# Scores' factor by Ln and Exp instead of Tanh and Square, fewer row copies, and another order of work between attention and experts

## What is computed

```python
qh, kh, vh = proj(q, Wq, bq), proj(k, Wk, bk), proj(v, Wv, bv)
scores = jnp.einsum('bhqd,bhkd->bhqk', qh, kh)
norm_q = jnp.linalg.norm(qh, axis=-1)
norm_k = jnp.linalg.norm(kh, axis=-1)
D_udps = (norm_q[..., :, None] + norm_k[..., None, :]) ** 2
scores = alpha * 4.0 * scores / D_safe          # D_udps, or inf where it is 0
attn = jax.nn.softmax(scores, axis=-1)
...
# experts: the best 2 of 8 for each token, weights by softmax
h = jax.nn.gelu(jnp.einsum('btd,edh->ebth', x, W1) + b1[:, None, None, :], approximate=False)
y = jnp.einsum('ebth,ehd->ebtd', h, W2) + b2[:, None, None, :]
out = jnp.einsum('ebtd,bte->btd', y, dispatch)
x = x + attention(layernorm(x), ctx, ctx); x = x + experts(layernorm(x))
```

## Time and profile before

| | |
|---|---|
| median of 3 runs | 966.4 us (966.29 to 967.87) |
| profiled execution | 970.74 us, of it 968.9 us in the profile's span |
| granted TensorE clock, mean | 0.977 of full |
| TensorE busy | 898.1 us, 93% |
| VectorE, ScalarE, GpSimd busy | 697.2, 634.5, 415.5 us |

### The profile page before, as it was taken

How to read it: one execution, slowest core, us unless ns; L and a number is a source line. 1 busy time by engine, 2 the same in 40 slices (tenths; PEclk the granted TensorE clock), 3 DMA queues, 4 the chain that set the end, 5 groups by cost and what they waited for, 6 DMA issues and landing times.

```text
span 968.9 us, 30634 instructions
## 1 busy us (share of the span) xinstructions
PE 898.1 (93%) x10701; PEld 789.8 (82%) x10701; DVE 697.2 (72%) x1833; ACT 634.5 (65%) x1236; POOL 415.5 (43%) x540
## 2 busy tenths in 40 slices
PE   3999999998999999989899699899999999999994
PEld 2788887787877877878777589799999999999993
DVE  7677888777987887779768577766666666666662
ACT  3688887787877877878857356455555455554551
POOL 6344456538546565385253532623222232222322
PEclk9799999999999999999979799999999999999998
DMA  5222122314132333253044773443333233332222
GB/s 150 70 72 89 41 83 80 112 41 128 57 99 76 126 123 103 92 171 111 20 139 134 275 273 52 85 93 52 51 52 51 47 52 52 52 51 48 46 30 22
DMA packets 61892, 84.82 MB, mean 88 GB/s; under 512 B 9872, under 2 KB 55312, under 8 KB 59568
## 3 DMA queue, kind: packets, MB, share of 16 engines
q1 hardware_dynamic: 47504, 64.26, 21.0%
q0 software_dynamic: 13296, 18.00, 11.1%
q10 hardware_dynamic: 944, 0.60, 0.2%
HBM read 49.86 MB, written 31.92 MB: 84 GB/s over the span
## 4 chain that ended last, share of the span: by engine, by line
PE 74%; issue 7%; DVE 6%; ACT 6%; POOL 3%; another core or an unknown queue 1%; DMA 1%; DVEq 0%; POOLq 0%; ACTq 0%
PE s_ps L711 10%; PE u_ps L711 10%; PE pv_ps L729 9%; PE gen L729 9%; PE gen L502 5%; PE gen L495 5%; PE s_ps L485 5%; PE u_ps L473 3%; PE pv_ps L519 2%; PE gen L544 2%; ACT pt L827 2%; PE gen L415 2%; PE gen L680 2%; PE gen L418 2%; PE gen L422 1%
## 5 line engine op out<-in xcount | busy, mean ns | idle before, releaser
L1567 POOL DMA_INDIRECT out<-yw,rb x71 | 110.3, 1553 | 269.4 <-DVE yw L1392 253.4
L928 ACT ACTIVATE h<-s_ps,b1t,inv 128x128 f32<-128x128 f32 x288 | 107.8, 457 | 89.6 <-PE s_ps L711 79.3
L928 ACT ACTIVATE h<-u_ps,b1t,inv 128x128 f32<-128x128 f32 x280 | 104.7, 459 | 87.4 <-PE u_ps L711 86.4
L1375 DVE TENSOR_SCALAR hs<-h,hsc 128x512 f16<-128x512 f32 x142 | 69.7, 491 | 120.4 <-ACT h L928 102.0
L827 ACT ACTIVATE pt<-gen,escale 128x512 f32<-128x512 f32 x128 | 86.8, 686 | 50.4 <-PE gen L502 34.5
L1377 DVE SCALAR_TENSOR_TENSOR hs<-h,hsc,hs 128x512 f16<-128x512 f32 x142 | 106.7, 751 | 5.1
L711 PE MATMUL s_ps<-xt,w1s 128*128 128x128 f16 x1728 | 104.8, 220 | 2.2 <-issue 2.2
L1517 POOL DMA_INDIRECT xrec<-rec,idx x64 | 77.8, 1215 | 60.9 <-DVE idx L1229 44.7
L711 PE MATMUL u_ps<-xt,w1s 128*128 128x128 f16 x1680 | 102.5, 220 | 0.9 <-issue 0.9
L711 PEld LDWEIGHTS s_ps<-xt,w1s 128*128 x1728 | 99.8, 99 | 2.8 <-issue 2.3
L729 PE MATMUL pv_ps<-w2s_sb,hs 128*128 x864 | 100.5, 272 | 0.5 <-issue 0.5
(11 more groups left out here) (251 smaller groups left out, 1741.8 us busy)
## 6 DMA issues: line engine op xcount, KB each, us to landing
wl<-L_ffn_W SPq DMA_DIRECT2D x16, 1024.0 KB
rb<-xrec SPq DMA_DIRECT2D x71, 132.5 KB
w2s<-wst SPq DMA_DIRECT2D x8, 1024.0 KB
w2s_sb<-w2s SPq DMA_DIRECT2D x8, 1024.0 KB, 20.4
xin<-x SPq DMA_DIRECT2D x32, 128.0 KB, 3.5
cin<-ctx SPq DMA_DIRECT2D x32, 128.0 KB, 2.1
xres<-x SPq DMA_DIRECT2D x32, 128.0 KB
out<-x SPq DMA_DIRECT2D x30, 128.0 KB, 2.0
```

The costliest lines, as they stand in the source:

```text
L928: ins = act.activation(h32[n % HBANKS][:, m % HB, :], hbank[n % HBANKS][:, o:o + SLOT], ACT.Gelu, scale=inv1[:, bass.ds(ex, 1)].bitcast(F3 ...
L1567: pool.indirect_dma_start(out[:, :], bass.IndirectOffsetOnAxis(ap=rb[j][:, D + NE:D + NE + 1], axis=0), yw[s % 2][:, :], None, compute_op= ...
```

## The change

- ScalarE's `factors` takes Ln of the norms' sum and then Exp of -2 times that, in place of Tanh and Square. `u_ps` now holds the sum of the norms, and the parts are those of the norms.
- `roots` replaces `norm_ln` and `norm_exp`: Ln of the summed squares with a tiny bias, directly followed by Exp(-0.5 x). VectorE's `norms` replaces `mantissas`, `logarithms` and `unit_coefficients`, and stands where `logarithms` stood, ahead of `weight_exponent`. GpSimd's `units` needs no coefficient any more and signals each block by itself.
- The four row copies become two, for both blocks together, and `flat_rows` has one wait. `heads_back` uses one product for all heads. `weight_exponent` writes its exponent without a copy.
- Between the loop and the experts: `take_records(0)` and `(1)` stand first on VectorE, the scales are split in two, `weight_low` of the last pair comes later, the addresses for `first_product` are computed ahead, three records are loaded first, and the second weights are loaded one after another (two under way) instead of all at once. The last pair's routing goes to later slots. A Gelu of one column stands before the first slot.

```diff
             def factors(n, p):
                 h = n % 2
                 act.wait_ge(*at(f"u{n}", p + 1))
...
-                act.activation(th[h][:, :], u_ps[:, :], ACT.Tanh, scale=0.5).then_inc(sig(f"th{n}"), 1)
+                act.activation(th[h][:, :], u_ps[:, :], ACT.Ln, scale=-0.5 / NORM_SCALE).then_inc(sig(f"th{n}"), 1)
                 act.wait_ge(*at(f"th{n}", p + 1))
-                act.activation(th[h][:, :], th[h][:, :], ACT.Square).then_inc(sig(f"t2{n}"), 1)
+                act.activation(th[h][:, :], th[h][:, :], ACT.Exp, scale=-2.0, bias=centre[:, :]).then_inc(sig(f"t2{n}"), 1)
...
-            def norm_ln(p):
-                act.wait_ge(*at("mant", p + 1))
-                act.activation(na["ln"][:, :, :], na["mant"][:, :, :].bitcast(F32), ACT.Ln).then_inc(sig("nln"), 1)
-
-            def norm_exp(p):
-                act.wait_ge(*at("ah", p + 1))
-                act.activation(na["y"][:, :, :], na["ah"][:, :, :], ACT.Exp, scale=-1.0).then_inc(sig("ny"), 1)
+            def roots(p):
...
+                act.activation(na["ln"][:, :, :], n2[:, :, :], ACT.Ln, bias=tiny[:, :]).then_inc(sig("nln"), 1)
+                act.wait_ge(*at("nln", p + 1))
+                act.activation(na["y"][:, :, :], na["ln"][:, :, :], ACT.Exp, scale=-0.5).then_inc(sig("ny"), 1)
...
+            def norms(p):
+
+                dve.wait_ge(*at("ny", p + 1))
+                step(dve.tensor_tensor(na["y2"][:, :, :], na["y"][:, :, :], na["y"][:, :, :], ALU.mult))
+                step(dve.scalar_tensor_tensor(na["n2y2"][:, :, :], n2[:, :, :], TINY, na["y2"][:, :, :],
+                                              ALU.max, ALU.mult))
+                step(dve.scalar_tensor_tensor(na["rn"][:, :, :], na["n2y2"][:, :, :], -3.0, na["y"][:, :, :],
+                                              ALU.add, ALU.mult))
+                step(dve.scalar_tensor_tensor(na["r1"][:, :, :], n2[:, :, :], TINY, na["rn"][:, :, :],
+                                              ALU.max, ALU.mult))
...
+                if p:
+                    dve.wait_ge(*dma("flat", 2 * NSPLIT * p))
+                dve.tensor_copy(kbr[:, :, :], both[:, :, 1, :]).then_inc(sig("rowk"), 1)
+                if p:
+                    dve.wait_ge(*at("u3", p))
+                dve.tensor_copy(aq[0:RROWS, :, :], both[:, :, 0, :]).then_inc(sig("rowq"), 1)
...
                 if 0 <= it + 1 < NP:
-                    logarithms(it + 1)
+                    norms(it + 1)
                 if 0 <= it < NP:
                     weight_exponent(it)
                 if 0 <= it + 1 < NP:
-                    unit_coefficients(it + 1)
                     rows(it + 1)
...
-            for s in range(U - 1):
+            for s in range(3):
                 load_records(s)
-            store_w2(NP - 1)
             sp.wait_ge(*at("pv3", NP))
-            for e in range(NE - 1):
-                load_w2(e)
-                if e == 0:
-                    sp.dma_start(b2s[:, :, :], b2.partition_broadcast(P)).then_inc(sig("ldb2"), 16)
-            sp.wait_ge(*dma("stw", NE))
-            load_w2(NE - 1)
+            load_w2(0)
+            sp.dma_start(b2s[:, :, :], b2.partition_broadcast(P)).then_inc(sig("ldb2"), 16)
+            for s in range(3, U):
+                load_records(s)
+            load_w2(1)
             for e in range(NE):
                 sp.wait_ge(*dma(f"ldw2_{e}", 1))
                 sp.sem_inc(sig("w2_ready"), 1)
+                if e == 3:
+                    store_w2(NP - 1)
+                    sp.wait_ge(*dma("stw", NE))
+                if e + 2 < NE:
+                    load_w2(e + 2)
...
+            take_records(0)
+            dve.tensor_scalar(inv1[:, :], k1[:, :], 25.0, float(ONE), ALU.subtract, ALU.mult).then_inc(sig("inv1"), 1)
+            take_records(1)
+            heads_back(1, NP - 1)
+            hidden_scales()
```

More of the change, by code:

```diff
@@ L381, in sync_program @@
                 sp.sem_inc(sig("w2_ready"), 1)
-            for s in range(U - 1, SOON):
+                if e == 3:
[3 more added lines that the diff above has]
+                    load_w2(e + 2)
+            for s in range(U, SOON):
                 load_records(s)
@@ L712, in first_product @@
                                             start=(t == 0), stop=(t == len(terms) - 1))
+                        for address in itertools.islice(ahead, 2 * DC):
+                            pe.to_reg(address)
                     ins.then_inc(sig("mm1"), 1)
@@ L915, in scalar_program @@
                     factors(1, it)
+            act.activation(gelu_one[:, :], mhalf[:, :], ACT.Gelu)
             def gelu(s):
@@ L1105, in rows @@
-            def rows(p):
-                gb = turn("rows_t", p)[:, :].bitcast(BF16)
-                dve.wait_ge(*at("rows_t", p + 1))
-                for b in range(2):
-                    if p:
-                        dve.wait_ge(*at(f"su{2 * b + 1}", p))
-                    dve.tensor_copy(aq[b][0:RROWS, :], gb[0:RROWS, 2 * b * P:(2 * b + 1) * P]).then_inc(sig(f"rowq{b}"), 1)
-                    if p:
-                        dve.wait_ge(*dma(f"flat{b}", NSPLIT * p))
-                    dve.tensor_copy(kbr[b][:, :], gb[0:RROWS, (2 * b + 1) * P:(2 * b + 2) * P]).then_inc(sig(f"rowk{b}"), 1)
+                step(dve.tensor_tensor(v4(na["r1"]), v4(na["r2"]), part(1), ALU.subtract))
@@ L1284, in weight_exponent @@
                 dve.wait_ge(*at("wcl", p + 1))
[L1285 to L1287 removed]
+                place = dst[:, p % NE:p % NE + 1]
+                exponent(wcl[:, :], place)
+                dve.tensor_scalar(wsc[:, :], place, -float(ONE), 268.0 * ONE, ALU.mult, ALU.add).then_inc(sig("wsc"), 1)
             for it in range(-2, NP + 3):
@@ L1393, in weigh, with hidden_scales @@
                                   None, ALU.mult).then_inc(sig("yw"), 1)
+            def hidden_scales():
+                exponent(b1ss[:, :], kb[:, :])
+                step(dve.tensor_scalar(mk[:, :], k1[:, :], 4.0, None, ALU.add))
+                step(dve.tensor_tensor(mk[:, :], mk[:, :], kb[:, :], ALU.max))
+                step(dve.tensor_scalar(mk[:, :], mk[:, :], 1.0, None, ALU.add))
+                step(dve.tensor_scalar(hsc[:, :], mk[:, :], -float(ONE), 268.0 * ONE, ALU.mult, ALU.add))
+                step(dve.tensor_tensor(inv2[:, :], mk[:, :], k2[:, :], ALU.add))
+                dve.tensor_scalar(inv2[:, :], inv2[:, :], 155.0, float(ONE), ALU.subtract, ALU.mult).then_inc(sig("scales"), 1)
+            take_records(0)
[3 more added lines that the diff above has]
+            hidden_scales()
+            experts = [expert_of(dve, s) for s in range(2)]
             residual(0, NP - 1)
-            heads_back(1, NP - 1)
-            take_records(0)
-            take_records(1)
-            experts = [expert_of(dve, s) for s in range(2)]
+            take_records(2)
             split_hidden(0, experts[0])
-            take_records(2)
+            split_hidden(1, experts[1])
             residual(1, NP - 1)
-            split_hidden(1, experts[1])
             for s in range(NSLOT):
```

240 lines of the change are left out of this document (105 added, 135 removed), and 2 rows, old and new, of the table TURNS.

## The result

The changed kernel takes 1120.4 us (median of 4 runs, 1119.8 to 1124.4), the kernel before 967.0 us beside it: ratio 1.160, 95% interval 1.157 to 1.162. It is 16% slower. The forecast, 1072 us, had the direction and the cause; the size was 48 us too small, and the time lies 10 us beyond the end of the range.

A forecast was written before the change was run, and what follows sets the result against it. The prediction took TensorE to bound the loop before and ScalarE, with its table loads, after. It summed +110 (15 iterations), +7.5 (the last) and -12 (step into the experts) to +105.5 on 966.4: 1072 us, range 1042 to 1110.

The forecast's parts named there:

- Ten loads an iteration: Attention loop, ScalarE: alternating Ln and Exp bring 10 table loads where there were 2, eight more costing 10.3 us an iteration.
- ScalarE's work: Attention loop: ScalarE's busy time rises from 26.06 to 36.3 us an iteration, over the 32.35 us an iteration took.
- First to third Ln: Part of an iteration on ScalarE: 11.0 us before, 14.1 after, with four more loads and nothing to wait for.
- the last iteration: The 16th, with no next pair to prepare: eight loads cost 10.3 us, some 2.8 cover old waits, +7.5.
- Third Ln to `pt`: Part of an iteration on ScalarE: 11.9 us before, 16.3 after, through `roots`, `norms`, `wcl` and TensorE's 12 products.
- The walk: ScalarE's queue followed from one iteration to the next in three segments, summing to 39.0 us, 39.7 with clock and scatters.
- from `pt` to the next first Ln: Part of an iteration on ScalarE: 7.9 us before, 8.6 after, with one more load and some old idle covered.
- The term of the sum: Attention loop: 39.7 less 32.35 is 7.35 us an iteration, times 15 iterations, +110 us.
- The lower clock: TensorE's pauses of 3 us in the loop bring a lower clock; 0.7 us an iteration added for this and scatters.
- Rival 1: More is exposed: pauses bring the lower clock, `turned` stands twice as long; 42 us an iteration, 1107 us; chance 0.11.
- The step into the experts: Between loop and experts: earlier record copy, addresses ahead and later slots for other work gain 12 us, bounds 6.5 and 14.
- Rival 2: One table serves Ln and Exp, no loads in the loop, up to five would be free: 940 us; chance 0.07.

The follow-up runs named there:

- one_set: Changed kernel plus one instruction loading the table that holds both Ln and Exp at ScalarE's start: ratio 1.0037 to the kernel before, 31.89 us an iteration.
- weights_route: weights_first plus the last routing's Exp moved from behind slot 6 to behind slot 7: ratio 1.138 to the kernel before, 40.08 us an iteration.
- after_beside: The changed kernel unaltered, run again on the chip of weights_route: ratio 1.170 to the kernel before, 41.61 us an iteration.
- weights_first: Changed kernel with the weights' step earlier on TensorE, in the bank ring and on VectorE, all 164 loads kept: ratio 1.143, 1092.9 us, 39.91 us an iteration.
- step_alone: Kernel before with only the part of the change behind the loop, the step into the experts: ratio 0.999.
- step_route: step_alone with the last routing's Exp on ScalarE moved from behind slot 6 to behind slot 7: ratio 0.994 to the kernel before.
- four_loads: one_set with a table load ahead of each Ln of `factors`, four an iteration: ratio 1.059 to the kernel before, 35.38 us an iteration.
- scores_first: Changed kernel with TensorE's fourth scores and first values ahead of `weight_products`, ScalarE's queue unchanged: ratio 1.151 to the kernel before, 41.1 us an iteration.
- eight_loads: one_set with a table load ahead of each Ln and each Exp of `factors`: ratio 1.147 to the kernel before, 1108 us.

## Why the prediction was right or wrong

- **Ten loads an iteration: right.** The reading of the earlier trace rows, that the table with Ln lacks Exp and the other way round, gave 64 and 64 loads on the two lines of `factors` and 164 in all ("about 165"). The Trainium skill's two pages, by which there would be none as the prediction read them, were rightly set aside for this program; that the joint table exists is right too (one_set).
- **ScalarE's work: right.** 36.3 us an iteration were forecast; from 112 to 500 us it is busy 339.9 of 388, 36.6 us in 41.73. Its share is 88%, not 90% or more, and TensorE's 83%, not 75 to 80.
- **First to third Ln, 14.1 us: right**, to 0.1 us (mean 14.0), and so is the last iteration, to 0.5 us (+8.0, forecast +7.5).
- **Third Ln to `pt`, 16.3 us: the step that failed.** It took 18.3 us in the mean of 15 iterations, mostly 18.1 to 19.5. The walk followed ScalarE's queue and one chain over VectorE, and both of these were nearly right: Exp of `roots` ends 12.8 us after the third Ln (forecast 12.65) and `wcl` is read at 15.6 (15.0). But it let TensorE be ready with its 12 products and put `pt` 1.3 us behind `wcl`. TensorE is not waiting for `wcl` at all: it stands 4.0 us in the ring of banks for ScalarE's copy of q and k, then has 8.2 us of its own queue to do at half clock, starts to turn the third tile 17.6 us after the third Ln, and needs 2.0 us for it instead of 1.1. Where the clock stays at 1.00, as in iteration 1, TensorE does wait for `wcl`, and `pt` comes after 16.3 us, the walk's own figure. The pause was shorter there too (1.5 us), so the two are not told apart by that one case; but they go together, and the queue alone is 2.4 us longer at the lower clock, or 3.5 without the waits in it.
- **Where the missing 2.0 us an iteration lie.** 41.73 instead of 39.7 is +2.0 in this segment and +0.8 from `pt` to the next first Ln (9.4 instead of 8.6), less the 0.7 allowed for clock and scatters. weights_route against after_beside, on one chip, shows that TensorE's queue behind the pause is worth 2.6 us of the segment and 1.5 of the iteration. That weights_first and weights_route then come to the forecast's 39.7 (39.9 and 40.1) is partly luck: their segment is 0.7 us shorter than the walk's 16.3, and the one behind it 1.7 longer than its 8.6 (10.3). What makes that last one longer wasn't tested.
- **The term of the sum:** 7.35 x 15 = +110 us was +143. It counts the difference from 32.35, the length of two iterations with a scatter, where the mean from first to last is 32.18; that is 2.6 us of the 33, the rest is the 2.0 us of the two points above.
- **The lower clock: right that it comes, mis-sized.** 0.7 us for it and the scatters was far too little: L491 takes 2.08 instead of 1.16 us, L585 1.86 instead of 1.08, and the queue from L585 to the third tile 2.4 us more than in iteration 1. The earlier trace rows was read for one stretch at 0.61; the next 4 us of that trace are at 0.50. Rival 1 (42 us an iteration, given 0.11) names this mechanism and comes to 1107 us; what it lacked is that not only `turned` but the whole queue behind the pause runs at half clock.
- **The step into the experts, -12: failed too.** It came to -0.2. The first product starts 8.7 us earlier, as forecast (8.5). But TensorE then stood 3.0 us, and the first product of the second slot took 4.47 us instead of 2.84 (granted clock 0.66 from 702 to 707 us), which leaves 8.5 us up to the first second product. And +8.3 came behind it, from a queue that the forecast didn't walk, ScalarE's with `route_exp` moved by one slot where `choose` moved by three. step_alone: nothing; step_route: -0.6%, so 5.7 of the 8.3 us; the rest is open.
- **The whole miss,** 153.7 instead of 105.5 us in the profiled span: 33 in 15 iterations, 0.5 in the last, 11.8 at the step into the experts, and 2.7 at the start, which the forecast had at nothing. In one_set, on another chip, the first Ln comes at 29.6 us instead of 33.8, so the loads ahead of it are the likely reason.
- **Rival 2, 940 without loads: wrong in its size.** one_set has no loads in the loop and is at 1.004. TensorE was busy 94% of the loop before, and so it is there; the time that ScalarE gives back it only waits. The rival's bound, that up to five loads an iteration are free as long as ScalarE's work stays under TensorE's 30.3 us, fell as well: in four_loads ScalarE has 28.7 us, and the loads cost 3.5 us.

## What to carry to other kernels

Look at which functions share a table in the trace of the kernel at hand, and count the loads that alternating calls bring, before pricing the functions; if a joint table exists, load it once by hand. When an engine becomes the bound, walk every queue that frees a buffer behind the place where it got longer, not the busiest one alone: here the waits were mutual, and of the seven smaller reorderings only scores_first gained anything (0.6 us an iteration, from another chip), until work was taken out of the queue behind the pause (1.5 us). Price a pause of TensorE not by its length but with the work that follows it at the lower clock. An order tuned for one bound is not neutral under another, so moved work must be timed in the kernel that will keep it.

## What the runs showed of the hardware

- Loading the table that is already loaded costs as much as changing it: 1.283 us each in four_loads and eight_loads as in the changed kernel.
- A pause of TensorE of 4.0 us at clock 1.00 was followed by 8 us at 0.50, although TensorE was busy through all of them (430 to 438 us); the 24 products of a slot took 4.25 instead of 2.78 us behind another pause of 4.0 us (changed kernel, 751.18 us). In the kernel before, a pause of 2.2 us was followed by 0.61 and then 0.50; behind the pause of 1.5 us of iteration 1 the clock stayed at 1.00.
- The price of a load was not constant, by medians: 0.83 us each for the first four an iteration, 1.35 for the next four, and roughly 0.4 to 0.7 for the two of `roots`, though each is 1.283 us long.
